# A recurrent stage's change of round: what is prepared early, what is done late, and who turns the final h

## The reference

```python
A = (adj != 0)
h = x
for l in range(5):
    m   = einsum('bnd,de->bne', h, weight[l])
    agg = einsum('bij,bid->bjd', A, m)
    # gru cell
    r = sigmoid(i_r + h_r); z = sigmoid(i_z + h_z)
    n = tanh(i_n + r * h_n)
    h = (1 - z) * n + z * h
x = layernorm(x + h * mask)
```

## Time and profile before

| | |
|---|---|
| median of three runs | 1141.59 us (1139.44 to 1142.74) |
| profiled execution | 1139.14 us, its span 1137.3 us |
| busy share of the span | PE 88%, DVE 79%, ACT 68%, POOL 64% |
| chain that ended last | PE 57%, DVE 19%, ACT 9%, issue 7%, POOL 3% |
| granted TensorE clock, mean | 0.967 |

### The profile page before, as it was taken

How to read it: one execution, slowest core, us unless ns; L and a number is a source line. 1 busy time by engine, 2 the same in 40 slices (tenths; PEclk the granted TensorE clock), 3 DMA queues, 4 the chain that set the end, 5 groups by cost and what they waited for, 6 DMA issues and landing times.

```text
span 1137.3 us, 21302 instructions
## 1 busy us (share of the span) xinstructions
PE 998.3 (88%) x6138; PEld 602.2 (53%) x6138; DVE 901.4 (79%) x2511; ACT 770.9 (68%) x1311; POOL 725.5 (64%) x751
## 2 busy tenths in 40 slices
PE   3699998495989998998998999899899999958884
PEld 2599998242344544454454454445445445547663
DVE  4599999373679878977977987897797798778996
ACT  1388887473667777776776777777677677726664
POOL 0589898293458657656855865765685685565553
PEclk9699999698999999999999999999999999979997
DMA  6133331234443432333333233242333333303323
GB/s 164 54 105 107 106 110 52 61 64 67 52 71 62 74 75 46 79 60 65 74 64 73 56 74 74 46 83 55 65 80 59 74 56 59 64 11 82 89 75 82
DMA packets 261150, 81.59 MB, mean 72 GB/s; under 512 B 188499, under 2 KB 260972, under 8 KB 261100
## 3 DMA queue, kind: packets, MB, share of 16 engines
q1 hardware_dynamic: 247274, 80.15, 32.3%
q10 hardware_dynamic: 13826, 0.85, 0.9%
HBM read 28.58 MB, written 8.81 MB: 33 GB/s over the span
## 4 chain that ended last, share of the span: by engine, by line
PE 57%; DVE 19%; ACT 9%; issue 7%; POOL 3%; ACTq 2%; DMA 1%; DVEq 0%; SPq 0%; POOLq 0%
PE psum L1198 15%; PE psum L1193 15%; PE psum L1194 15%; PE psum L1222 6%; DVE st L816 4%; DVE x L827 2%; PE psum L1281 2%; ACT psum L727 2%; DVE mv L820 2%; ACT rt L749 2%; DVE ws L963 2%; ACTq L703 2%; PE psum L1236 2%; DVE ot L1105 2%; PE psum L1296 1%
## 5 line engine op out<-in xcount | busy, mean ns | idle before, releaser
L587 POOL TENSOR_TENSOR zh<-zw,ht 128x512 f32<-128x512 f32 x160 | 203.6, 1272 | 102.5 <-ACT zw L752 80.6
L560 POOL TENSOR_TENSOR htp<-ht,htp 128x512 f16<-128x512 f32 x128 | 149.1, 1165 | 117.2 <-ACT htp L738 117.2
L1193 PE MATMUL psum<-htp,wh_hi 128*128 128x512 f16 x480 | 182.6, 380 | 39.3 <-ACT rt L749 24.9
L1193 PE MATMUL psum<-pth,wx_hi 128*128 128x512 f16 x480 | 183.3, 382 | 13.8 <-ACT pth L712 13.6
L1198 PE MATMUL psum<-ptl,wx_hi 128*128 128x512 f16 x480 | 183.3, 382 | 4.1 <-DVE ptl L1012 3.2
L1194 PE MATMUL psum<-pth,wx_lo 128*128 128x512 f16 x480 | 183.2, 382 | 0.0
L1198 PE MATMUL psum<-htp,wh_hi 128*128 128x512 f16 x480 | 182.4, 380 | 0.0
L1194 PE MATMUL psum<-htp,wh_lo 128*128 128x512 f16 x480 | 182.4, 380 | 0.0
L752 ACT ACTIVATE zw<-psum,brz,unscale 128x512 f32<-128x512 f32 x160 | 124.4, 777 | 67.2 <-PE psum L1198 67.2
L993 DVE SCALAR_TENSOR_TENSOR rt<-psum,bhn,rt 128x512 f32<-128x512 f32 x160 | 119.6, 748 | 57.8 <-ACT rt L749 55.7
L712 ACT ACTIVATE pth<-psum 128x512 f16<-128x512 f32 x160 | 95.6, 597 | 93.1 <-PE psum L1222 77.3
(11 more groups left out here) (162 smaller groups left out, 1844.4 us busy)
## 6 DMA issues: line engine op xcount, KB each, us to landing
adj<-in_adj_dram SPq DMA_DIRECT2D x32, 256.0 KB, 2.9
x<-in_x_dram SPq DMA_DIRECT2D x32, 256.0 KB, 3.3
adjr<-in_adj_dram SPq DMA_DIRECT2D x32, 256.0 KB, 3.0
out_dram<-yo SPq DMA_DIRECT2D x8, 768.0 KB
hnp<-htp SPq DMA_TRANSPOSE x128, 3.1
out_dram<-xq SPq DMA_DIRECT2D x32, 50.0 KB
v<-in_L_gnn_W_dram SPq DMA_DIRECT2D x2, 640.0 KB, 5.3
x3q<-x SPq DMA_DIRECT2D x16, 50.0 KB
```

Source lines behind the costliest of these rows:

```text
L560: nc.gpsimd.tensor_tensor(HT_LO[s % 2], HT[s][:, :], HT_HI[s % 2], ALU.subtract).then_inc(b_htl, 1)
L587: nc.gpsimd.tensor_tensor(ZH[s % 2][:, :], ZW[s % 2][:, :], HT[s][:, :], ALU.mult).then_inc(b_zh, 1)
L1193: mm(dst, w_h[:, col:col + P], h[:, :], start=start, stop=False)
```

## The change

It touches stage B alone, and the waits of stage C that go with it.

- x pair: four tiles instead of two (`X_OF`). Streams 0 and 1 are made a round ahead: ACT's half at lag -16, at the end of ACT's slot, DVE's at lag -15. Streams 2 and 3 stay at lag 0. `run_b` begins 16 slots earlier, and the first two rounds are unrolled.
- A16 moves from lag 0 to lag -2, the second pair of adjacency loads from lag 0 to lag -1.
- The final h is no longer transposed by PE. ACT makes its high half (lag 4, in front of the R sigmoid), POOL its low half (lag 4, in front of L587), SP turns the pair by a DMA transpose (lag 4), and POOL sums it into YB (lag 7).
- The tail is spread: mask at lag 11, add at 15, statistics at 16, aggregates at 18, rstd and two small operations for the negated mean at 19, applies at 20, two by DVE and two by ACT. The division by `UP_H` goes into the mask.
- DVE's order in a slot is now: Cq, x low half, A16, aggregates, statistics, applies, L993, L1000, L1007, L1012. POOL's: low half of h, L571, low half of the final h, L587, sum of the turned pair, mask, add, rstd.
- SP's x transpose now itself waits for N(h) of two items before (b_hn) and for the L571 of two groups before. The final pair's transpose waits also for the sum of two groups before (b_ye).

```diff
@@ SP
+                x = at(-1)
+                if x and x[0] == 0 and x[1] < 2:
+                    sp.wait_ge(b_a16, gth(x))
+                    load_b(x[1] + 2, x[2])
...
+                    if l == 0:
+                        sp.wait_ge(b_sxl, gth(x))
+                        reach(sp, b_hn, nth(x) - 2)
+                        reach(sp, b_h0, gth(x) - 2)
+                        sp.dma_start_transpose(blocks(HTP[p]), X_OF[s][:, :]).then_inc(b_tr[p], 16)
...
+                x = at(4)
+                if x and x[0] == L - 1:
+                    sp.wait_ge(b_fl, gth(x))
+                    reach(sp, b_ye, gth(x) - 2)
+                    sp.dma_start_transpose(blocks(FNP[p]), FTP[p][:, :]).then_inc(b_tf[p], 16)
@@ POOL, behind L587 (lag 2)
+                x = at(7)
+                    pool.wait_ge(b_tf[s % 2], turned_last(x))
+                    nc.gpsimd.tensor_tensor(YB[s][:, :], hi, lo, ALU.add).then_inc(b_ye, 1)
+                x = at(11)
+                    # mask, as before
+                x = at(15)
+                    wait_apart(pool, b_ym, gth(x))
+                    nc.gpsimd.tensor_tensor(YB[s][:, :], YB[s][:, :], of_group(x2, x), ALU.add).then_inc(b_y, 1)
+                x = at(19)
                     rstd(MVB[s][:, :], VEB[s], RSB[s][:, :], G4, b_mv, gth(x), b_ve, b_rs)
+                    # NMB = mean * rstd, then * -1
@@ ACT, behind the Z sigmoid
+                x = at(-16)
+                if x and x[0] == 0 and x[1] < 2:
+                    reach(act, b_at, nth(x) - TURN)
+                    nc.scalar.activation(halves(X_OF[s])[0], of_group(x2, x), ACT.Copy, scale=UP_H).then_inc(b_sxh, 1)
+                x = at(20)
+                    wait_apart(act, b_nm, gth(x))
+                    # two applies, then b_x3h
@@ DVE, behind Cq (lag 4) and ahead of L993 (lag 3)
+                for lag, some in ((-15, (0, 1)), (0, (2, 3))):
+                    x = at(lag)
+                    if x and x[0] == 0 and x[1] in some:
+                        dve.wait_ge(b_sxh, gth(x))
+                        nc.vector.scalar_tensor_tensor(lo, of_group(x2, x), UP_H, hi, ALU.mult, ALU.subtract)\
+                          .then_inc(b_sxl, 1)
+                x = at(-2)
                 if x and x[0] == 0:
                     dve.wait_ge(b_lda[s % 2], it * (16 * STREAMS // 2) + 16 * (s // 2 + 1))
                     reach(dve, b_at, nth(x) - STREAMS)
                     # A16
+                x = at(18)
+                    # aggregates, behind b_bs
+                x = at(16)
+                    wait_apart(dve, b_y, gth(x))
+                    # statistics
+                x = at(20)
+                    wait_apart(dve, b_rs, gth(x))
+                    # two applies
@@ PE
-                y = at(4)
-                if y and y[0] == L - 1:
-                    pe.wait_ge(b_h, nth(y))
-                    for i in range(G4):
-                        last = nc.tensor.transpose(cols(T_B, i), cols(HT[y[1]], i), ident[:, :])
-                    last.then_inc(b_tp, 1)
```

More of the change, by code:

```diff
@@ L175, in graph_stack_kernel @@
         RSB = [sb(f"rsb{s}", [P, G4]) for s in range(STREAMS)]
+        NMB = [sb(f"nmb{s}", [P, G4]) for s in range(STREAMS)]
         sbb = ExitStack()
@@ L574, in slot_b @@
                     l, s, it = x
[L575 to L578, removed]
+                    hi, lo = halves(FTP[s % 2])
+                    pool.wait_ge(b_fh, gth(x))
+                    nc.gpsimd.tensor_tensor(lo, HT[s][:, :], hi, ALU.subtract).then_inc(b_fl, 1)
                 x = at(2)
@@ L713, in slot_b @@
                 x = at(0)
-                if x and x[0] == 0:
+                if x and x[0] == 0 and x[1] >= 2:
                     l, s, it = x
[L716 to L720, removed]
+                    reach(act, b_at, nth(x) - STREAMS)
+                    nc.scalar.activation(halves(X_OF[s])[0], of_group(x2, x), ACT.Copy, scale=UP_H).then_inc(b_sxh, 1)
                 x = at(3)
@@ L741, in slot_b @@
                     l, s, it = x
-                    act.wait_ge(b_tp, gth(x))
-                    nc.scalar.activation(YB[s][:, :], T_B, ACT.Copy, scale=1.0 / UP_H).then_inc(b_ye, 1)
+                    act.wait_ge(b_h, nth(x))
+                    reach(act, b_tf[s % 2], turned_last(x) - 16)
+                    nc.scalar.activation(halves(FTP[s % 2])[0], HT[s][:, :], ACT.Copy).then_inc(b_fh, 1)
                 x = at(2)
@@ L753, in slot_b @@
                                          bias=brz[:, 1:2], scale=unscale[:, 1:2]).then_inc(b_z, 1)
+                x = at(-16)
+                if x and x[0] == 0 and x[1] < 2:
+                    l, s, it = x
+                    reach(act, b_at, nth(x) - TURN)
+                    nc.scalar.activation(halves(X_OF[s])[0], of_group(x2, x), ACT.Copy, scale=UP_H).then_inc(b_sxh, 1)
+                x = at(20)
+                if x and x[0] == L - 1:
+                    l, s, it = x
+                    wait_apart(act, b_nm, gth(x))
+                    for i in range(G4 // 2):
+                        last = nc.scalar.activation(
+                            x2[:, bass.ds(it * (STREAMS * G4 * D) + (s * G4 + i) * D, D)], cols(YB[s], i),
+                            ACT.Identity, bias=NMB[s][:, i:i + 1], scale=RSB[s][:, i:i + 1])
+                    last.then_inc(b_x3h, 1)
                 x = at(0)
@@ L973, in slot_b @@
             def slot_b(at):
[L974 to L980, removed]
                 x = at(4)
@@ L1219, in slot_b @@
                     reach(pe, b_pl, n - 1)
-                    for h, half in enumerate((HN_HI[p], HN_LO[p])):
+                    for h, half in enumerate(halves(X_OF[s] if l == 0 else HNP[p])):
                         for i in range(G4):
```

145 lines of the change are left out of this document (80 added, 65 removed).

## The result

The changed kernel takes 1557.28 us in the median of four runs (1554.62 to 1561.08), beside 1141.4 for the kernel before: a ratio of 1.3648, interval 1.3613 to 1.3683. The profiled execution's span is 1552.6 us, 415.3 longer than the 1137.3 of before.

The account below looks back on a forecast made before the run. PE, busy 88%, was taken as the bound, losing time only where it waits. 1139.1 - 55 + 338 (waits) + 9.5 (round 0) + 1.5 (start) + 16 (end) + 42 (clock) = 1491, median 1493 us; range 1400 to 1560.

Parts of the forecast that it names:

- The likeliest case: Recurrent stage: DVE stalls ahead of r times N, with PE's clock mixed; 1493 us, chance 0.55.
- if the span rises by more than the 350 us that the waits give: Whole span: a larger rise than 350 us was named as a sign that the prediction is wrong.
- Slots 12 to 19: DVE's statistics and applies wait for POOL's add and rstd: +4.2 and +4.0 us per slot, 16.9 and 15.9 per round.
- the clock's term: Slots 12 to 19: four tenths of the time at 1.2 GHz, 1.9 us per slot then, 42 us over 56 slots.
- Slots 0 and 1: DVE's A16 waits for PE's P of this slot: +1.5 us each, 3.0 per round.
- Slots 2 to 6: DVE's x low half waits for ACT, 5.9 us in slots 2 and 3; slots 4 to 6 lose 6.6 together.
- The SP step: Final pair's transpose waits for POOL's sum, delaying the x transpose behind it; slots 4 to 6 lose 6.6 us.
- Clock low in every stalled slot: Rival for slots 12 to 19: all 56 stalled slots pay the lower clock; 1556 us, chance 0.13.
- The waits are met: Rival: DVE stands a slot or more behind POOL, change slots fall to 4.34 us; 1109 us, chance 0.07.
- Clock kept: Rival: the stalls come but PE's clock stays full; 1451 us, chance 0.13.
- Only part of it binds: Rival: only the eight POOL-fed slots stall, neighbours' slack catches up the rest; 1335 us, chance 0.11.
- -55 us: Slots where a round changes and the one after: 7.9 us won at each of seven changes.

Follow-up runs that it names:

- the filler: Changed kernel plus fourteen unused PE matmuls between Z(h) and N(h) in slots 12 to 19 of every round from the second on: 1507.0 us, 1.319 of before.
- the run with the sum alone: Changed kernel with only POOL's sum of the turned final pair moved from lag 7 to lag 5: 1543.46 us, 1.354 of before.
- the first experiment: Changed kernel with x low half, A16, statistics and applies on DVE all one lag later: 1208.74 us, 1.0586 of before.
- the second: Changed kernel with all those DVE consumers one lag later and POOL's sum at lag 5 instead of 7: 1149.39 us, 1.0072 of before.
- the third: Changed kernel with DVE's late work behind P's low half, statistics at lag 17, applies at 21, sum at lag 5: 1132.54 us, 0.9918 of before.

## Why the prediction was right, and where its numbers fell short

**The sign and the mechanism** stand. The likeliest case, stalls of DVE ahead of L1083 with a mixed clock, is what the trace shows and what the lags undo. "PE's share down to about 68%" came out as 71%, "DVE's idle time ahead of the statistics and the applies, [...] of some 4 us x 28 each" as 149.4 (14.1 of them in the tail) and 107.0 us, and PE's idle stands ahead of N(h) and not ahead of R(h). The sign of being wrong, "if the span rises by more than the 350 us that the waits give", did come true, by 65. It stood at the forecast itself, which adds up to 352 with the clock, so it couldn't tell much; but it asks where the 65 are.

**Sum against the trace**, in the spans' own time (predicted 352 with the clock, measured 415.3):

| part | predicted | measured |
|---|---|---|
| start | +1.5 | +0.95 |
| round 0 | +9.5 | +11.95 |
| seven rounds, change slots and clock in | 338 - 55 + 42 = 325 | +389.0 |
| tail, last P to the end | +16 | +13.4 (149.4 to 162.8) |

So the start and the end were sized well. (In the end DVE's last stage began 25.05 us after the last h, from 1396.91 + 0.69 to 1422.65; predicted 26.) The miss lies in the seven rounds, 9.1 us each. By the P intervals of the round from 498.20:

- **Slots 12 to 19**: predicted 67.4 at full clock plus 6.1 for the clock, 73.5; measured 75.8. The stall was right, 8.46 for 8.55 where the clock was full, and 68.3 for 67.4 over the eight with the filler: 0.9 of the miss. The rest, 1.4, is the clock's term, 6.1 for the 7.5 between the two windows of 75.80 and 68.33. Miss: 2.3.
- **Slots 0 and 1**: predicted 5.84 each; measured 6.63 and 6.71, at a clock of 1.00. A16 was costed at 0.35 to the next start, from its row of before, and took 1.31 in its new place, beside L609. The row was right and the place was not. Miss: 1.7.
- **Slots 2 to 6**: predicted 34.1, measured 39.55. The x low half was costed at 0.61 to the next start, 0.69 by itself, and three of the four in a round took 1.3 to 1.6. The line in the trace after, for streams 2 and 3 (minimum, median and maximum in ns), and three of the four instructions of the round from 648.54, of which the third was not lengthened:

```profile
L1046 DVE SCALAR_TENSOR_TENSOR hnp<-x,hnp x16: 692/1408/1578, 224.3 to 1259.2; 128x512 f16<-128x512 f16 x10, 128x512 f16<-128x512 f32 x6
```

```profile
650.54 1.40 DVE L1046 SCALAR_TENSOR_TENSOR hnp<-x,hnp 128x512 f16<-128x512 f16 x1 [3.21 <-ACT hnp L764]
...
658.54 1.58 DVE L1046 SCALAR_TENSOR_TENSOR hnp<-x,hnp 128x512 f16<-128x512 f16 x1 [3.12 <-ACT hnp L764]
...
671.29 0.69 DVE L1046 SCALAR_TENSOR_TENSOR hxp<-x,hxp 128x512 f16<-128x512 f16 x1 [2.61 <-ACT hxp L803]
```

  The first two, beside POOL's L594, give 1.6: where the clock stood at 1.00, slots 2 and 3 are 8.09 and 7.88, together 1.5 over twice the predicted 7.26. The clock, which I had put at full in these slots and which was 0.87 over them, takes 1.5 more in slot 3, 9.42 here for the 7.88 of the round from 949.13. Slots 4 to 6, 22.0 for 19.6, hold the remaining 2.4; the last x low half, 1.31 at 681.99, and the clock are in it, and no run takes these apart. Miss: 5.4.

2.3, 1.7 and 5.4 make 9.4 in this round, against 9.1 in the mean. The failed steps are thus two durations taken from where an instruction stood before, though the change moved it beside another engine's instruction, and a clock term confined to eight slots of a round.

**The SP step** was right in kind. In the third group's case after, the sum ran until 668.85, and SP and PE show what followed (time to issue; PE's wait in brackets):

```profile
668.92 1.23 SPq L490 DMA_TRANSPOSE fnp<-ftp  x1
670.25 1.27 SPq L480 DMA_TRANSPOSE htp<-hnp  x1
673.45 0.61 PE L1255 MATMUL psum<-htp,wh_hi 128*128 128x512 f16 x1 [3.63 <-DMA htp<-hnp]
```

The final pair's transpose was issued 0.07 us behind the sum, the x transpose behind it, and PE waited 3.63 us for its landing. The prediction had given slots 4 to 6 a loss of 6.6 and let it take in the x waits of slots 5 and 6; the run with the sum alone shows that the two do share their time: while the x waits stand, the sum's edit gives 14 us and not 59.

**The clock.** The row of 0.80 at 52% busy stood for a share of four tenths at the lower level. Over the eight slots the clock is 0.86, so 0.28 at the lower level and not 0.4; yet the cost is larger, since it doesn't fall evenly. Windows after, of three stretches of matmuls behind a wait and, third, of a wait:

```profile
563.92:567.88 3.96, 3.42 (x16) 1.32 (x16) 2.43 (x4) 2.45 (x4) 1.16 (x1) 1.00 0.01 4
581.88:587.24 5.36, 4.82 (x15) 1.71 (x16) 2.71 (x8) 2.48 (x4) 1.15 (x1) 0.68 0.07 15
587.24:591.75 4.51, 1.26 (x13) 0.65 (x11) 1.58 (x6) 0.93 (x2) 2.48 (x2) 1.00 0.22 41
591.75:597.29 5.54, 5.00 (x15) 1.76 (x16) 2.71 (x8) 2.58 (x4) 1.15 (x1) 0.69 0.11 23
```

The same sixteen or so matmuls take 3.96 us at 1.00 and 5.4 to 5.5 at 0.68, and the wait between, which gains nothing by a fast clock, has 1.00. Low clock times length says little until one sees on what it falls. In each of rounds 1 to 6 two of the eight stalled slots keep 1.00 and six pay; in the round shown the first one is among the two, in four others it pays. The Trainium skill (TensorE: Matmul & The Clock Gate, "HAM oscillation — how this bites in real kernels") tells of a kernel in which the work behind each such wait is slow. That is nearer to this than my even mixture, yet at the row's 1.9 us it would have come to 105 us in the 56 slots, where the filler measures 50.

**The rivals.** "Clock low in every stalled slot" gave 1556, next to the measured 1557, for the wrong reason: its 105 us of clock were 50, and the rest of its sum is the two lengthened instructions and the clock of other slots. That the range held the result, by 3 us, is luck in the same way: its upper end stood for those 105 us. "The waits are met" named 1109, and the kernel in which they are met takes 1107, though with the sum earlier and without the loop's jumps as well. "Clock kept", 1451, is below the 1507 of the filler run, since that run still has the lengthened instructions, and the lowered clock in slots 2 to 5. "Only part of it binds" fell: every named place stalled.

**What the change is worth.** Between the changed kernel and the one that does the same operations in better places lie, in medians (the second and the last on the other chip):

| step | us |
|---|---|
| changed kernel | 1557.3 |
| statistics and applies a lag later | 1324.4 |
| x low half and A16 a lag later as well | 1208.7 |
| sum at lag 5 | 1149.4 |
| DVE's late work at the end of its slot | 1132.5 |
| DVE's rounds written out | 1107.0 |

Most of the -55 us that the change could win were there too: in the last of these the seven rounds and round 0 are 45 us shorter than before (the time from first to last P is 721.6 us, it was 766.8), and the tail gives 14 back.

**What stays open.** Why DVE's loop seems to be fetched again at its jump in some kernels; the count of pieces and the run without a loop speak for that, no view shows the fetch itself. The stops are there in all four in which the applies stand at lag 21 and the loop is kept (53 pieces in each; by PE's intervals they cost 15 us in the first experiment, 17 in the second, 24 in the third), and not after the change, in the run with the sum alone or in that with the added matmuls, all with lag 20 (33 pieces). In the code, lag 21 makes the first slot of a round reach two rounds back instead of one; all four also have the statistics at lag 17. Whether one of these, the loop's length or its place decides wasn't tried. Nor was a version with a shorter tail.

## What to carry to other kernels

Where in-order engines walk through slots, a lag is not an age: ask at which end of its slot the producer makes its result and at which end of its own the consumer wants it, since one slot too few at the head of an engine's list cost 349 of 1557 us here and no operation. Take a duration from a row only if the instruction keeps its neighbours; beside a GpSimd operation of 128x512, A16 took three times as long. When a fix moves less than its sum says, look for a wait that has taken its place, and at the idle time called "issue" at a loop's jump.

## What the runs showed of the hardware that I had not expected

- A VectorE tensor_scalar of 128x512 (f32 to f16) took 0.42 us alone or beside a GpSimd operation of 128x4, and 1.31 to 1.36 (medians of two kernels) where most started beside one of 128x512; a scalar_tensor_tensor with two SBUF inputs 0.69 and up to 1.58. Those with a PSUM input stayed at 0.67 to 0.75 in all kernels.
- Matmuls put into a wait made the kernel faster: 784 of them, -50 us, with a granted clock of 1.00 in the slots instead of 0.86.
- A VectorE loop that had run without a stop stood for up to 5.8 us at its jumps in the kernels whose applies had lag 21, and the instruction queue moved 20 more pieces; written out, with 7 more pieces than after the change, it had no stop.
